# A gated cross-attention block with experts: units in three runs, four score tiles each with one maximum, then the full-precision products together; output weights in one load

## The chip, the cores and the metric

One core of a Trainium2 chip runs the whole kernel. The metric is the device time of one execution in microseconds (us); lower is better. Before the change three executions took 336.08, 337.61 and 337.05 us, median 337.05 us.

## The reference

The block has two halves. The first is cross-attention from 8 x 56 query tokens (width 128) to 8 x 1500 context tokens, with 16 heads of width 8, behind a layer norm and a tanh gate:

```
q = norm(x) @ w_q.T ; k = ctx @ w_k.T ; v = ctx @ w_v.T      # 16 heads of 8
attn = softmax(q k^T * 8**-0.5) ; out = (attn v) @ w_o.T
x = x + tanh(g_xattn) * out
```

The second is a mixture of 8 experts (inner width 512), of which a router picks two for every token; all eight are computed for all 448 tokens and combined with weights that are zero for the others:

```
probs = softmax(h @ gate_w.T) ; top 2, renormalised -> combine
gu = h @ gate_up_w ; out = sum_e combine_e * (up_e * gelu(gate_e)) @ down_e
x = x + tanh(g_ffn) * out
```

Everything is float32. The softmax of the first half needs the maximum of each (query, head) row, which the kernel computes by products of its own.

## The kernel before, in words

The kernel is written by hand for the five engines, each with its own program, tied by semaphores. There is no scheduler: the order on an engine is the order of the code.

**Units.** Attention works in 16 units, u = 0 to 15: a batch b (8 of them) times a half h of the heads (8 heads each). A unit has 12 score tiles of 128 keys; a tile is 128 x 448 (8 heads x 56 queries), made by two matmuls of 224 columns each (L880, `score_ps`), from keys `kx` as weights and block-diagonal queries `qx`. Keys and queries are split in a high and a low part in a rounded format (fp32r), stacked over the rows, so that one fast matmul does what three would. Rows 96 to 103 of `qx` carry the negated maxima against rows of ones in `kx`, so the score matmul subtracts the maximum.

**What an instruction is.** `scores` makes score tiles; in this version two tiles (a pair) per step. `max_scores` (L905) makes one of the 12 products of a unit, 112 query rows x 512 keys, from which `take_max` on VectorE (L664) takes the row maximum. After 12 of them `negate_max` (L670, L672, L674) makes `neg_max_parts`, `transpose_max` (L928) on TensorE transposes them, and `max_rows` (L683) on VectorE writes them to `qx`. `exp_pair` (L480) on ScalarE does the exponential of a pair (896 columns) to `probs`. `attend` (L919) multiplies four tiles of `probs` with the values: 16 matmuls, each in two passes of the trace (x32), in full precision (fp32), four heads side by side in 32-column groups of the array. `o_copy` (L488) takes the sum of a unit out of PSUM to `o_sb`, `denominators` (L936) spreads the sums of the exponentials, `invert` (L691) inverts them, and `normalise` (L377, GpSimd) multiplies. `project` (L862 for keys, L868 for values) does a third of the key or value projection of a batch that comes later, in full precision, through the one bank `misc_ps`; ScalarE evacuates it (L459 and L462 for keys, L474 for values) and GpSimd makes the low part of the keys (L351, `k_rest`).

**Work ahead.** While unit u is scored and attended, the maxima of unit u+1 are finished and those of unit u+2 begun. All products for maxima, the transpose and the denominators go through a ring of two PSUM banks, `max_ps`: a turn waits until VectorE has taken the turn two before it (`next_bank`). Four banks hold scores (two pairs), one `o_ps`, one `misc_ps`.

**Keys move.** The projected keys of a batch are moved by 12 DMAs from SP's queue (`move_keys`, L230) to two slots of `kx`, six per unit, when all three parts of `k_low` are done (L273) and the unit that used the slot has been scored. ScalarE waits in `keys_moved` for these copies before it overwrites `k_high` and `k_full` with the next batch's keys. In the prologue ScalarE's queue issues six of them. The output weights `wo_sb` are zeroed on VectorE (L700) and filled by 16 DMAs from GpSimd's queue (L370).

**The end.** Units 12 to 15 are unrolled; 13 to 15 have no projections, 14 no later maxima, 15 none. Between units 13 and 14 stands `project_out` of three quarters of the tokens (L1060). After unit 15 come the output projection of the rest, the router and the experts.

Of the kernel before, what the change touches and what calls it, by code (L numbers as in the profile page):

```python
# [33 lines left out]
PAIRS = KT // 2  # L34
TRIOS = KT // 4
UM = NCH * HP
RING = UM + 2
RING0 = UM + 6
# [19 lines left out]
def flamingo_block(nc, x, ctxT, g_attn, g_ffn, wqT, wkT, wvT, woT, gwT, guT, dnT, out):  # L58
# [3 lines left out]
    with ExitStack() as stack:  # L62
# [20 lines left out]
        probs = sb("probs", [128, 4, 2, SC // 2])  # L83
# [56 lines left out]
        hact = probs[:, 0:2, :, :].rearrange("p a b t -> p (a b) t")  # L140
# [9 lines left out]
        q_banks = [max_ps[:, 0, :], max_ps[:, 1, :], score_ps[:, 3, :], o_ps[:, :]]  # L150
        token_banks = [misc_ps[:, D * r:D * r + D] for r in range(NR)]
        xT_ps = max_ps[:, 0, :]
        gate_banks = [score_ps[:, 0, :], score_ps[:, 1, :]]
        up_banks = [score_ps[:, 2, :], misc_ps[:, :], score_ps[:, 3, :]]
# [9 lines left out]
        consts, mask_ready, select_all, cleared, wo_cleared, pool_step = map(sem, ("consts", "mask_ready", "select_all", "cleared", "wo_cleared", "pool_step"))  # L164
# [70 lines left out]
        def _(sp):  # L235
# [21 lines left out]
            sp.dma_start(kx[MR:KR, 0, 1, :].bitcast(f32), kx[MR:KR, 0, 0, :].bitcast(f32)).then_inc(ones_moved, 16)  # L257
            ones_rows(1)
# [6 lines left out]
            move_unit(1, 1)  # L265

            def body(i, par, ctx_next=True):
# [5 lines left out]
                sp.wait_ge(scores_done, PAIRS * (2 * b + 1))  # L273
                move_unit(par, 0)
                sp.wait_ge(scores_done, PAIRS * (2 * b + 2))
# [21 lines left out]
        def _(pool):  # L297
# [66 lines left out]
            pool.wait_ge(wo_cleared, 1)  # L364
            for s in range(2):
                for i in range(2):
                    for j in range(4):
                        h = 2 * (4 * s + j) + i
                        r = 32 * j + HD * i
                        pool.dma_start(wo_sb[r:r + HD, 2 * s + i, :], woT[HD * h:HD * h + HD, :]).then_inc(wo_loaded, 16)  # L370

            def normalise(i, par, h, turn=RING - 1):

# [8 lines left out]
            def body(i, par):  # L382
                b = batch(i, par)
                pool.wait_ge(scores_done, PAIRS * 2 * b + 1)
                stage(b + 1, 1 - par, 1)
                k_rest(b + 2, 0)
                normalise(i, par, 0)
                k_rest(b + 2, 1)
                k_rest(b + 2, 2)
                pool.wait_ge(scores_done, PAIRS * (2 * b + 1))  # L390
                stage(b + 2, par, 0)
                normalise(i, par, 1)
# [4 lines left out]
            pool.wait_ge(scores_done, PAIRS * (NU - 4) + 1)  # L397
# [18 lines left out]
            normalise(3, 1, 0, 8)  # L416
            for made, (kind, e) in enumerate(FIRST_WEIGHTS[:-1]):
                if made == 2:
                    normalise(3, 1, 1, 9 - RING)
                weights_rest(kind, e, e % 2, made + 1)  # L420
# [26 lines left out]
        def _(act):  # L447
# [6 lines left out]
            nc.scalar.activation(scratch[:, :], scratch[:, :], ACT.Exp).then_inc(exp_done, 1)  # L454
# [21 lines left out]
            def exp_pair(i, par, h, k):  # L476

                act.wait_ge(scores_done, PAIRS * unit(i, par, h) + k + 1)
                slot, bank = (PAIRS * h + k) % 4, 2 * (k % 2)
                nc.scalar.activation(probs[:, slot, :, :], score_ps[:, bank:bank + 2, 0:SC // 2],  # L480
                                     ACT.Exp, scale=SCALE).then_inc(exp_done, 1)

            def o_copy(i, par, h):

                u = unit(i, par, h)
                act.wait_ge(o_norm_ready, u + 1)
                act.wait_ge(pv_done, TRIOS * (u + 1))
# [20 lines left out]
            act.wait_ge(g_loaded, 32)  # L508
# [712 lines left out]
```

## Time and profile before

| | us |
|---|---|
| median of three executions | 337.05 |
| the profiled execution | 337.0 |
| its span | 335.3 |
| TensorE busy with matmuls | 294.7 (88%) |
| TensorE busy with weight loads | 223.0 (67%) |
| VectorE busy | 236.3 (70%) |
| ScalarE busy | 183.0 (55%) |
| GpSimd busy | 101.3 (30%) |

The span runs from the first to the last recorded instruction; the profiled execution's time is 1.7 us longer. TensorE's busy time counts a matmul from its start to its modelled end, so that one matmul's time overlaps the next; the step from start to start, or the chain of waits, says what a group of matmuls really takes. In the chain, every piece is the work or the wait that the next piece stood behind, so its pieces add up to the time that passed.

### The profile page before, as it was taken

To read this page: it belongs to the slowest core of one execution; us is meant where nothing else is said; L and a number is where in the kernel's file an instruction comes from. 1 tells how busy PE (TensorE), PEld (TensorE's weight loads), DVE (VectorE), ACT (ScalarE), POOL (GpSimd) and SP (SyncE) were. 2 spreads that over 40 slices of the span, in tenths; PEclk is the share of its full clock that TensorE was granted. 3 is DMA by queue.
4 is the path that set the end of the run, shared out by engine and by line. 5 is a ranking of instruction groups with operands and counts; after the bars stand their busy time and mean duration, and the time that the engine had idled before them with its cause. 6 is when DMAs were issued, how large, how long until landed. Compare 5 with 4: busy or idle time off the path is not lost.

```text
span 335.3 us, 7712 instructions
## 1 busy us (share of the span) xinstructions
PE 294.7 (88%) x2793; PEld 223.0 (67%) x2793; DVE 236.3 (70%) x429; ACT 183.0 (55%) x284; POOL 101.3 (30%) x124
## 2 busy tenths in 40 slices
PE   0949799999999999999999999898668899999875
PEld 0535586686686686687687686676556688887653
DVE  3534778778777778777777778866233788888874
ACT  1512367566566566566665664445616577775422
POOL 6021952311411411321320330000441066664330
PEclk9985899999999999999999999999956999999979
DMA  5498572197098098099087079300000000000000
GB/s 161 137 225 100 142 179 96 24 212 230 6 214 243 0 206 254 0 196 254 13 182 187 0 170 262 129 0 2 2 0 1 2 1 0 0 0 0 0 0 29
DMA packets 10379, 32.33 MB, mean 96 GB/s; under 512 B 2976, under 2 KB 3616, under 8 KB 10360
## 3 DMA queue, kind: packets, MB, share of 16 engines
q1 hardware_dynamic: 8840, 30.59, 36.8%
q10 hardware_dynamic: 1008, 1.42, 1.8%
q8 instruction: 12, 0.20, 0.2%
q0 software_dynamic: 512, 0.07, 0.1%
q14 instruction: 7, 0.06, 0.1%
HBM read 13.06 MB, written 0.23 MB: 40 GB/s over the span
## 4 chain that ended last, share of the span: by engine, by line
PE 67%; DVE 20%; issue 4%; POOL 2%; ACT 2%; DMA 2%; ACTq 1%; DVEq 0%; SPq 0%
PE max_ps L905 17%; PE o_ps L919 13%; DVE part_max L664 10%; PE score_ps L880 9%; PE misc_ps L868 5%; PE score_ps L1105 4%; PE misc_ps L862 3%; PE score_ps L1106 3%; PE score_ps L1107 3%; PE score_ps L862 2%; DVE kx L829 2%; DVE k_low L810 2%; DMA ctx_sb<-in_ctxT 2%; DVE probs L824 2%; POOL kx L404 1%
## 5 line engine op out<-in xcount | busy, mean ns | idle before, releaser
L664 DVE TENSOR_REDUCE part_max<-max_ps 112x1 f32<-112x512 f32 (+1 forms) x192 | 127.9, 674 | 53.9 <-PE max_ps L905 50.4
L480 ACT ACTIVATE probs<-score_ps 128x896 f32<-128x896 f32 x96 | 87.5, 918 | 52.2 <-PE score_ps L880 50.9
L905 PE MATMUL max_ps<-kx,qx 96*112 96x512 f32 (+1 forms) x192 | 92.7, 487 | 8.8 <-DVE part_max L664 7.2
L880 PEld LDWEIGHTS score_ps<-qx,kx 104*128 104x128 f32 (+1 forms) x384 | 56.4, 191 | 6.0 <-ACT probs L480 2.3
L880 PE MATMUL score_ps<-qx,kx 104*128 104x224 f32 (+1 forms) x384 | 59.8, 279 | 0.6 <-ACT probs L480 0.3
L351 POOL TENSOR_TENSOR k_low<-k_full,k_high 128x512 fp32r<-128x512 f32 (+1 forms) x21 | 26.2, 1251 | 110.2 <-ACT k_full L462 110.2
L905 PEld LDWEIGHTS max_ps<-kx,qx 96*112 96x112 f32 x192 | 34.5, 181 | 30.4 <-DVE part_max L664 25.4
L919 PE MATMUL o_ps<-probs,v_sb 128*32 128x112 f32 (+1 forms) x1536 | 46.6, 262 | 0.0
L919 PEld LDWEIGHTS o_ps<-probs,v_sb 128*32 128x32 f32 (+1 forms) x1536 | 35.3, 110 | 11.0 <-issue 9.1
L404 POOL TENSOR_TENSOR kx<-gu_sb,kx 128x512 fp32r<-128x512 f32 x16 | 23.1, 1446 | 38.4 <-ACT kx L562 38.4
L596 ACT ACTIVATE kx<-probs 128x448 fp32r<-128x448 f32 x32 | 18.5, 577 | 23.4 <-DVE probs L824 22.7
L868 PE MATMUL misc_ps<-wv_sb,ctx_sb 128*128 128x128 f32 x192 | 28.0, 293 | 3.2 <-ACT v_sb L474 3.2
L868 PEld LDWEIGHTS misc_ps<-wv_sb,ctx_sb 128*128 128x128 f32 x192 | 27.2, 207 | 5.3 <-ACT v_sb L474 4.1
L829 DVE TENSOR_TENSOR kx<-probs,kx 128x448 fp32r<-128x448 f32 x32 | 23.1, 721 | 0.3
L566 ACT ACTIVATE v_sb<-score_ps 128x448 f32<-128x448 f32 x32 | 17.2, 540 | 7.5 <-PE score_ps L1107 7.1
L824 DVE TENSOR_TENSOR probs<-score_ps,v_sb 128x448 f32<-128x448 f32 x24 | 14.9, 620 | 8.9 <-PE score_ps L1107 8.9
L474 ACT ACTIVATE v_sb<-misc_ps 128x512 f32<-128x512 f32 x24 | 14.4, 599 | 10.0 <-PE misc_ps L868 10.0
L862 PE MATMUL misc_ps<-ctx_sb,wk_sb 128*128 128x512 f32 (+1 forms) x38 | 19.0, 580 | 0.0
L377 POOL TENSOR_TENSOR o_norm<-o_sb,inv_den 128x112 f32 (+1 forms) x16 | 6.7, 421 | 39.2 <-DVE inv_den L691 39.2
L223 POOL TENSOR_TENSOR qx<-q_parts,head_mask 96x448 fp32r<-96x448 f32 x15 | 13.9, 931 | 10.5 <-DVE q_parts L710 10.2
L691 DVE RECIPROCAL inv_den<-max_ps 128x112 f32<-128x112 f32 x16 | 13.6, 849 | 4.6 <-PE max_ps L936 4.4
L488 ACT ACTIVATE o_sb<-o_ps 128x112 f32<-128x112 f32 x16 | 4.2, 263 | 21.3 <-PE o_ps L919 21.3
(148 smaller groups left out, 388.6 us busy)
## 6 DMA issues: line engine op xcount, KB each, us to landing
kx<-k_high SPq DMA_DIRECT2D x56, 187.5 KB, 3.9
ctx_sb<-in_ctxT SPq DMA_DIRECT2D x7, 750.0 KB, 6.3
kx<-k_low SPq DMA_DIRECT2D x28, 187.5 KB, 4.0
gu_sb<-in_guT SPq DMA_DIRECT2D x8, 512.0 KB, 4.7
dn_sb<-in_dnT SPq DMA_DIRECT2D x8, 256.0 KB, 5.3
kx<-k_high ACTq DMA_DIRECT2D x4, 187.5 KB, 5.5
ctx_sb<-in_ctxT SPq DMA_DIRECT2D x2, 256.0 KB, 6.7
kx<-k_high SPq DMA_DIRECT2D x4, 123.5 KB, 4.6
```

The costliest lines, as they stand in the source:

```text
L351: nc.gpsimd.tensor_tensor(k_low[:, start:start + size], k_full[:, start:start + size], k_high[:, start:start + size].bitcast(f32), ALU.sub ...
L404: nc.gpsimd.tensor_tensor(weight_parts[:, kind, par, 1, :], weights_of(kind, e), weight_parts[:, kind, par, 0, :].bitcast(f32), ALU.subtra ...
L480: nc.scalar.activation(probs[:, slot, :, :], score_ps[:, bank:bank + 2, 0:SC // 2], ACT.Exp, scale=SCALE).then_inc(exp_done, 1)
L596: nc.scalar.activation(hact_parts[:, j, 0, :], hact[:, j, :], ACT.Copy).then_inc(hact_high, 1)
L664: nc.vector.reduce_max(part_max[:, p, c:c + 1], max_ps[0:PC, bank, 0:size], AX.X).then_inc(max_taken, 1)
L824: nc.vector.tensor_tensor(hact[:, j, :], up_banks[j % NB][:, 0:TOK], gelu_sb[:, par, j, :], ALU.mult).then_inc(hact_full, 1)
L829: nc.vector.tensor_tensor(hact_parts[:, j, 1, :], hact[:, j, :], hact_parts[:, j, 0, :].bitcast(f32), ALU.subtract).then_inc(hact_ready, 1)
L862: nc.tensor.matmul(bank[:, 0:size], wk_sb[:, :], ctx_sb[:, par, start:start + size], start=True, stop=True).then_inc(k_done, 1)
L868: last = nc.tensor.matmul(misc_ps[:, 128 * k:128 * k + 128], ctx_sb[:, par, 128 * t:128 * t + 128], wv_sb[:, :], start=True, stop=True)
L880: last = nc.tensor.matmul(score_ps[0:m, t % 4, GC * g:GC * g + GC], kx[0:KR, 2 * par + h, g, 128 * t:128 * t + m], qx[0:KR, par, 2 * h + g ...
L905: nc.tensor.matmul(max_ps[0:PC, bank, 0:size], qx[0:MR, par, 2 * h + p // 2, PC * (p % 2):PC * (p % 2) + PC], kx[0:MR, slot, p // 2, start ...
L919: last = nc.tensor.matmul(o_ps[32 * j:32 * j + 32, PC * h:PC * h + PC], v_sb[0:m, par, t, VP * p:VP * p + 32], probs[0:m, (PAIRS * h + t / ...
```

## The change

In the loop of attention, each unit is now three runs. A run is four times (one score tile, one maximum product), then the full-precision products: a third of a projection, and the attend of the four tiles. The denominators of the unit before stand behind the first run, the transpose of the maxima of unit u+1 in the second, between projection and attend. The maxima of unit u+2 that are made ahead are six instead of five. Score tiles are counted one by one (`exp_tile` on ScalarE, 448 columns), with three score banks instead of two pairs; the maximum ring has three banks instead of two, so a turn waits for the turn three before it. `probs` keeps eight tiles, as before. The transpose counts for two turns, so the ring stays a multiple of three (15 turns per unit instead of 14).

Projections stand elsewhere: the last two value parts of batch b+1 in runs 1 and 2 of the even unit, key parts 0, 1, 2 of batch b+2 in run 3 of the even unit and runs 1 and 2 of the odd one, and the first value part of b+2 in its run 3. On GpSimd `stage` and one `k_rest` come ahead of `normalise`. In the prologue the keys of the second unit are moved from SP's queue, not ScalarE's, value projections stand later, and the first key projections of batch 1 use the three score banks. The output weights arrive already laid out (the zeros included, made on the host from the same matrix) and are one DMA of SP's queue.

```
-PAIRS = KT // 2
+RUN = 4
+RUNS = KT // RUN
-RING = UM + 2
+AHEAD = UM // 2
+RING = UM + 3
...
-        score_ps = pb("score_ps", [128, 4, 512])
-        max_ps = pb("max_ps", [128, 2, 512])
+        score_ps = pb("score_ps", [128, 3, 512])
+        max_ps = pb("max_ps", [128, 3, 512])
...
-            def exp_pair(i, par, h, k):
+            def exp_tile(i, par, h, t):
+                act.wait_ge(scores_done, KT * unit(i, par, h) + t + 1)
+                nc.scalar.activation(probs[:, (KT * h + t) % 8, :], score_ps[:, t % 3, 0:SC // 2],
                                      ACT.Exp, scale=SCALE).then_inc(exp_done, 1)
...
             def attention(i, par, h, after=True):                       # VectorE
-                for n in range(5, UM):
-                    take_max(ring(u, n - 5), (n - 5) % 2, n)
-                negate_max(u + 1, ring(u, UM - 5))
+                for n in range(RUN):
+                    take_max(ring(u, n), n % 3, AHEAD + n)
+                invert(u - 1, 1 - h, ring(u, RUN), RUN % 3)
+                for n in (5, 6):
+                    take_max(ring(u, n), n % 3, AHEAD + n - 1)
+                negate_max(u + 1, ring(u, 7))
...
-            def scores(i, par, h, k, rows=0):
+            def scores(i, par, h, t, rows=0):                            # TensorE
+                pe.wait_ge(exp_done, KT * unit(i, par, h) + t + FIRST_EXP - 2)
...
             def next_bank(turn):
-                pe.wait_ge(max_taken, turn - 1)
+                pe.wait_ge(max_taken, turn - 2)
...
+                scores(i, par, h, 0, rows)
+                next_max(6, 0)
+                scores(i, par, h, 1)
+                next_max(7, 1)
+                scores(i, par, h, 2)
+                next_max(8, 2)
+                scores(i, par, h, 3)
+                next_max(9, 3)
+                denominators(u - 1, 1 - h, ring(u, RUN), RUN % 3)
+                job(0)
+                attend(i, par, h, 0)
+                scores(i, par, h, 4)
+                next_max(10, 5)
+                scores(i, par, h, 5)
+                next_max(11, 6)
+                scores(i, par, h, 6)
+                later_max(0, 7)
+                scores(i, par, h, 7)
+                later_max(1, 8)
+                job(1)
...
+                    transpose_max(u + 1, ring(u, 9), 0, turns=2)
                 attend(i, par, h, 1)
+                for t in range(2 * RUN, KT):
+                    scores(i, par, h, t)
+                    later_max(t - 6, t + 3)
+                job(2)
                 attend(i, par, h, 2)
...
-                act.wait_ge(k_low_saved, NCH)
-            for g in range(2):
-                move_keys(act, 1, 1, g, (0, TK), kx_loaded[1][g])
...
+            sp.dma_start(wo_sb[:, :, :], wo).then_inc(wo_loaded, 16)
```

TensorE's order in the loop before the change, second half of an even unit. `REGISTER_ALU` computes the value of a wait; one row of x4 score matmuls is a pair of tiles, `max_ps<-kx,qx` is a maximum, `o_ps<-probs,v_sb` an attend, `misc_ps` a projection:

```order
L919 MATMUL o_ps<-probs,v_sb 32x112 x16
L892 REGISTER_ALU
L905 MATMUL max_ps<-kx,qx 112x476
L880 MATMUL score_ps<-qx,kx 128x224 x2
L880 MATMUL score_ps<-qx,kx 92x224 x2
...
L905 MATMUL max_ps<-kx,qx 112x512
L946 REGISTER_ALU
L868 MATMUL misc_ps<-wv_sb,ctx_sb 128x128 x4
L926 ISA
L892 REGISTER_ALU
L928 MATMUL max_ps<-ident,neg_max_parts 8x112
```

One or two maxima stand between any two full-precision products here. After the change, a whole run (the second of the first odd unit in the loop), with L871 a score tile, L891 a maximum, L854 a key projection, L914 the transpose and L905 the attend:

```order
L871 MATMUL score_ps<-qx,kx 128x224 x2
L878 REGISTER_ALU
L891 MATMUL max_ps<-kx,qx 112x512
L868 REGISTER_ALU
L871 MATMUL score_ps<-qx,kx 128x224 x2
...
L938 ISA
L854 MATMUL misc_ps<-ctx_sb,wk_sb 128x476
L912 REGISTER_ALU
L878 REGISTER_ALU
L914 MATMUL max_ps<-ident,neg_max_parts 8x112
L900 REGISTER_ALU
L905 MATMUL o_ps<-probs,v_sb 32x112 x16
```

The rounded products stand four and four together, and projection, transpose and attend follow each other.

VectorE's order in the loop before, from the last maximum of unit u+1 on:

```order
L664 TENSOR_REDUCE part_max<-max_ps 112x1 [waits max_done]
L670 TENSOR_REDUCE neg_max<-part_max 112x4 [waits max_taken]
...
L674 TENSOR_TENSOR neg_max_parts<-neg_max,neg_max_parts 112x4 [waits nm_step]
L676 REGISTER_ALU
L663 REGISTER_ALU [waits nm_step]
L664 TENSOR_REDUCE part_max<-max_ps 112x1 [waits max_done]
L680 REGISTER_ALU
L683 TENSOR_TENSOR qx<-max_ps,pair_mask 8x448 [waits max_done]
```

and after, in the same place (L653 is the maximum, L672 writes the transposed maxima to `qx`):

```order
L663 TENSOR_TENSOR neg_max_parts<-neg_max,neg_max_parts 112x4
L665 REGISTER_ALU
L652 REGISTER_ALU [waits nm_step]
L653 TENSOR_REDUCE part_max<-max_ps 112x1 [waits max_done]
L652 REGISTER_ALU
L653 TENSOR_REDUCE part_max<-max_ps 112x1 [waits max_done]
L669 REGISTER_ALU
L672 TENSOR_TENSOR qx<-max_ps,pair_mask 8x448 [waits max_done]
```

Two maxima instead of one now stand between the negation and the write to `qx`, and the denominators' inverse has moved from the unit's end to the place behind the first four maxima of the next unit.

## Rows read from the trace of the kernel before

**Rows 1.** The page: TensorE's granted clock in 40 slices, tenths of full speed

```profile
PEclk9985899999999999999999999999956999999979
```

**Rows 2.** Timeline of ScalarE, ends of units: start us, us, what [idle before]

```profile
52.11 0.26 ACT L488 ACTIVATE o_sb<-o_ps 128x112 f32<-128x112 f32 x1 [1.44 <-PE o_ps L919]
...
193.36 0.26 ACT L488 ACTIVATE o_sb<-o_ps 128x112 f32<-128x112 f32 x1 [1.09 <-PE o_ps L919]
...
218.27 0.26 ACT L488 ACTIVATE o_sb<-o_ps 128x112 f32<-128x112 f32 x1 [2.21 <-PE o_ps L919]
...
231.67 0.26 ACT L488 ACTIVATE o_sb<-o_ps 128x112 f32<-128x112 f32 x1 [1.24 <-PE o_ps L919]
...
239.73 0.26 ACT L488 ACTIVATE o_sb<-o_ps 128x112 f32<-128x112 f32 x1 [1.26 <-PE o_ps L919]
```

**Rows 3.** Chain of waits within one unit: start us, us, what

```profile
142.99 0.89 PE misc_ps L868 x8
...
147.29 0.44 PE score_ps L880 x4
147.73 0.22 PE max_ps L905
147.95 0.90 PE o_ps L919 x32
148.85 0.42 PE max_ps L905
...
153.42 0.49 PE max_ps L905
```

**Rows 4.** The page, section 5: weight loads of the maximum products, idle time before them

```profile
L905 PEld LDWEIGHTS max_ps<-kx,qx 96*112 96x112 f32 x192 | 34.5, 181 | 30.4 <-DVE part_max L664 25.4
```

**Rows 5.** Busy us in 129.18:141.99 and 141.99:154.88, two units; sum and mean

```profile
sum 25.70, PE 24.88 PEld 18.76 DVE 19.67 ACT 16.31 POOL 6.37; mean PE 12.44 PEld 9.38 DVE 9.83 ACT 8.15 POOL 3.19
```

**Rows 6.** Timeline of TensorE in unit 14

```profile
223.45 0.38 PE L905 MATMUL max_ps<-kx,qx 96*112 96x476 f32 x1
223.66 0.60 PE L880 MATMUL score_ps<-qx,kx 104*128 104x224 f32 x4
...
226.58 0.49 PE L905 MATMUL max_ps<-kx,qx 96*112 96x512 f32 x1
226.91 0.60 PE L880 MATMUL score_ps<-qx,kx 104*128 104x224 f32 x4
```

**Rows 7.** Timeline of VectorE in one unit

```profile
157.63 0.85 DVE L691 RECIPROCAL inv_den<-max_ps 128x112 f32<-128x112 f32 x1
...
164.80 0.17 DVE L670 TENSOR_REDUCE neg_max<-part_max 112x4 f32<-112x12 f32 x1
...
165.49 0.69 DVE L664 TENSOR_REDUCE part_max<-max_ps 112x1 f32<-112x512 f32 x1
166.21 0.62 DVE L683 TENSOR_TENSOR qx<-max_ps,pair_mask 8x448 fp32r<-8x448 f32 x1
```

**Rows 8.** Timeline of ScalarE: activations of 448 columns, two in a row and one alone

```profile
252.66 0.98 ACT L566 ACTIVATE v_sb<-score_ps 128x448 f32<-128x448 f32 x2
254.78 0.54 ACT L566 ACTIVATE v_sb<-score_ps 128x448 f32<-128x448 f32 x1 [1.14 <-PE score_ps L1107]
```

**Rows 9.** SP's DMA issues of one batch's keys, first and last; page, median landing

```profile
142.29 0.52 SPq L230 DMA_DIRECT2D kx<-k_high  x1
...
151.18 0.94 SPq L230 DMA_DIRECT2D kx<-k_high  x1
...
kx<-k_high SPq DMA_DIRECT2D x56, 187.5 KB, 3.9
```

**Rows 10.** Timelines of ScalarE and GpSimd: a key copy, the low part of keys

```profile
156.78 0.60 ACT L459 ACTIVATE k_high<-misc_ps 128x512 fp32r<-128x512 f32 x1 [0.18 <-PE misc_ps L862]
...
166.67 1.20 POOL L351 TENSOR_TENSOR k_low<-k_full,k_high 128x476 fp32r<-128x476 f32 x1 [4.32 <-ACT k_full L462]
```

**Rows 11.** Timeline of the prologue: weight loads of a value projection

```profile
22.48 1.78 PEld L868 LDWEIGHTS misc_ps<-wv_sb,ctx_sb 128*128 128x128 f32 x8 [3.47 <-ACT v_sb L474]
```

More of the change, by code:

```diff
@@ L362, in _, with normalise @@
                 k_rest(1, n)
[L364 to L372, printed above, removed]
+            def normalise(i, par, h, turn=RING + RUN):
                 u = unit(i, par, h)
@@ L543, in attention @@
                 o_copy(i, par, h)
-                if not last:
-                    exp_pair(*ahead(i, par, h, 1), 0)
-                if job_next:
-                    evacuate(*ahead(i, par, h, 1), 0)
             with act.Fori(0, B // 2 - 1) as i:
@@ L657, in k_rest, with take_max @@
                                         ).then_inc(k_low_saved, 1)
-            def take_max(turn, bank, n, first=False):
+            def take_max(turn, bank, n, first=False, turns=1):
                 p, c = max_product(n, first)
@@ L676, in negate_max, with max_rows @@
                 dve.wait_ge(nm_step, 3 * v + 3)
-            def max_rows(turn, bank, par, h):
+            def max_rows(turn, bank, par, h, turns=1):
                 dve.wait_ge(max_done, turn + 1)
@@ L723, in _ @@
             for n in range(UM):
-                take_max(n, n % 2, n, first=True)
+                take_max(n, n % 3, n, first=True)
             negate_max(0, UM)
             take_max(UM, 0, 0)
-            max_rows(UM + 1, 1, 0, 0)
-            for n in range(1, 5):
-                take_max(UM + 1 + n, (n + 1) % 2, n)
+            take_max(UM + 1, 1, 1)
+            max_rows(UM + 2, 2, 0, 0)
+            for n in range(2, AHEAD):
+                take_max(UM + 1 + n, (1 + n) % 3, n, turns=3 if n == AHEAD - 1 else 1)
             nc.vector.tensor_copy(expert_sel[:, :, :], bc(row_mask[:, :].unsqueeze(2), [16, E, 128])).then_inc(select_all, 1)
@@ L902, in max_scores @@
                     pe.wait_ge(kx_loaded[slot][n // 6], MOVES * (i + 1))
-                if not first or n >= 2:
+                if not first or n >= 3:
                     next_bank(turn)
@@ L1012, in attention @@
+            transpose_max(0, UM + 2, 2)
+            for n in range(2, AHEAD):
+                max_scores(0, 0, 1, n, UM + 1 + n, (1 + n) % 3, turns=3 if n == AHEAD - 1 else 1)
+            pe.wait_ge(k_saved, 4 * NCH)
+            pe.wait_ge(ones_moved, 64)
+            def attention(i, par, h, rows, jobs=(0, 1, 2), after=True):
                 u = unit(i, par, h)
                 u1, u2 = ahead(i, par, h, 1), ahead(i, par, h, 2)
-                def next_max(n):
-                    max_scores(*u1, n, ring(u, n - 5), (n - 5) % 2)
@@ L1044, in attention @@
[L1044 to L1054 removed]
+                        max_scores(*u2, n, ring(u, turn), turn % 3)
@@ L1199, with heads_apart @@
     layout = np.ascontiguousarray
+    def heads_apart(rows):
+        blocks = np.zeros((4, 32, 4, D), np.float32)
+        for s in range(2):
+            for i in range(2):
+                for j in range(4):
+                    h = 2 * (4 * s + j) + i
+                    blocks[j, HD * i:HD * i + HD, 2 * s + i] = rows[HD * h:HD * h + HD]
+        return blocks.reshape(128, 4, D)
     arrays = {
```

317 lines of the change are left out of this document (141 added, 176 removed).

## The prediction, made before the change was run

> **What bounds the kernel now.** I read the page's busy shares and clock first, then the timeline of ScalarE for the unit boundaries, then the chain of waits through one unit, then the timelines of TensorE, VectorE and ScalarE around it, and last the DMA queue. TensorE is busy for 88% of the span, VectorE 70%, ScalarE 55%, as the table above has it; the clock row stands at 9 from the sixth slice up to the end of attention, the full 2.4 GHz level but for a few us [rows 1]. The copy of a unit's output (o_sb) marks its end: 16 units, of which five are shown: 0, 11, 13, 14 and 15, at 52.11, 193.36, 218.27, 231.67 and 239.73 us [rows 2]. From unit 0 to unit 11 lie 11 periods in 141.25 us: **12.84 us per unit**. What follows the last copy (335.3 - 239.7 = 95.6 us: router, experts, store) is hardly touched. The profiled execution took 337.0 us, 1.7 us more than its span, and stands at the median of 337.05.
>
> Where do 12.84 us go? I add TensorE's own work in a unit from the chain of waits [rows 3], where a step is the time until the next can follow:
> - six score pairs at 0.44: 2.64
> - twelve maxima at 0.23: 2.76
> - three attends (o_ps x32) at 0.90: 2.70
> - three projections at 0.89 (the key ones 0.86): 2.61
> - behind each attend the next product takes 0.42 and not 0.23, since its weight load is not hidden: 3 x 0.19 = 0.57
> - transpose and denominators, about 0.2 each: 0.4
>
> Sum 11.7 us. The other **1.15 us are TensorE waiting for VectorE**: a maximum that comes back from such a wait stands in the chain with 0.49 instead of 0.23, as in its last row [rows 3], and page section 5 names the waiter: weight loads of L905 idled 30.4 us in all, 25.4 of it for part_max L664, that is 25.4 / 16 = 1.6 us per unit with the ends [rows 4]. VectorE is not full: 9.83 us busy in a unit [rows 5]. It waits for TensorE and TensorE for it in turns, because two maximum banks hold only one product ahead, and because the negation (three small steps) is followed by one more maximum and the transpose in the same narrow place.
>
> **The change, run by run.** A unit becomes three runs of four (score tile, maximum), each followed by the full-precision products, as the two excerpts of TensorE's order show. TensorE's columns stay what they were: the same 24 score matmuls, 12 maxima, 3 projections, 3 attends. Price of one (tile, maximum): 0.22 + 0.23 = 0.45; the one place where a maximum stands between scores on both sides shows it (223.45 to 223.66 for a 476-column maximum, then 0.44 for four score matmuls) [rows 6]. So a run is 4 x 0.45 = 1.8, plus 0.19 behind the attend ahead of it, plus 0.88 projection, plus 0.90 attend, plus 0.2 in two of three runs: again 11.7 us.
>
> The waits, walked. A maximum takes VectorE 0.69 [rows 7], a little less for 476 columns, 0.67 on average; I estimate that it starts about 0.2 after its product's last column.
> - Run 1: products end at 0.6, 1.1, 1.5, 2.0; VectorE is free of them at 1.5, 2.1, 2.8, 3.5. The denominators need the second bank: wait 0.1 to 0.2. invert 0.85 [rows 7] ends at 4.3, beside projection and attend (until 4.2).
> - Run 2: two maxima until 6.2, then the negation: 0.17 three times with gaps, 0.7 from 164.80 to 165.49 [rows 7], until 6.9. TensorE reaches the transpose at 6.9: wait 0 to 0.1. Then two maxima until 8.2 and max_rows 0.62 [rows 7] until 8.9, beside the attend.
> - Run 3: begins at about 8.1; its second maximum needs the bank of the transpose, free at 8.9, and comes at 9.0. The last maxima are taken by 11.5, before run 1 fills again.
>
> Waits 0.3 us instead of 1.15: **12.0 us per unit**, a gain of 0.84. VectorE's 9.83 us of work would fill 82% of that, so it doesn't bound.
>
> ScalarE: twelve exps of 448 columns instead of six of 896. Alone, 448 columns take 0.54 and two in a row 0.98, so the second adds 0.44 [rows 8]. Per unit that is 5.3 to 6.5, with the copies some 3 more, in 12: ScalarE is busy 8.15 now [rows 5] and becomes no bound. The attend waits for the fourth exp of its run, at 0.4 + 4 x 0.54 = 2.6 in the worst case; TensorE gets there at 2.0 + 0.88 = 2.9. The projection hides it. Where there is no projection, it doesn't (below).
>
> Key copies: L230 moves begin when k_low is done, 12 DMAs, first 142.29, last 151.18, and 3.9 us to land: 12.8 us [rows 9]. In the new order the last key chunk is projected at 6.9 of the odd unit, copied (0.6 + 0.5) and rounded on GpSimd (1.2 [rows 10]) by about 9.2; the copies land at 22.0. ScalarE needs them ahead of the next key copy at about 10.3 + 12 = 22.3. That is 0.3 us of slack plus roughly 0.8 that ScalarE can be late before TensorE feels it. I cost it at nothing and keep its price as a rival.
>
> Units without projections (13, 14, 15): TensorE stalls at each attend for exps, but has 2.6 less work. Unit 13: run = 0.4 + 4 x 0.45 (exp) + 0.1 + 0.90 + 0.2 = 3.4, and VectorE 9.8 over all; about 11.0. Unit 12 still has two projections: 11.8. The two took 24.9 (193.36 to 218.27): -2.1. Unit 14 has only six maxima, and the output projection: about 12.6 against 13.4: -0.8. Unit 15 had score pairs running ahead of the attends and took 8.06 [rows 2]; now scores 4 to 7 stand behind attend 0, so each run is 3.2 to 3.3: 9.6, **+1.5**.
>
> Prologue: ScalarE issued six key DMAs ahead of the first value copy, and TensorE idled 3.47 for that copy until 22.48 [rows 11]. That goes, but the keys of the first unit still have to land, and the clock's half level (1.2 GHz, the 8, 5 and 8 in the third to fifth slice [rows 1]) covers the same work. I take -1.0, bounds -3 and +1.5 (the second unit's keys now queue on SP behind the first's, six issues of 0.5 to 0.9 as in [rows 9]). The 16 wo_sb DMAs leave GpSimd's queue; what stood behind them, a qx that is read two units later, has time: nothing, at most -0.5. The one DMA in their place stands on SP behind 12 key moves, ahead of the first ctx load in the loop: one issue, nothing.
>
> **Sum**: -1.0 (prologue), 11 x -0.84 = -9.2, -2.1, -0.8, +1.5: together -11.6. 337.0 - 11.6 = 325.4 profiled, and as median **325.4 us**. Its own bounds: the waits 0 to 0.6 per unit (13 units: -4 to +4), the prologue: 321 to 329.5.
>
> **A rule against the row.** The chain shows 0.42 behind an attend against 0.23 behind scores [rows 3], an exposed weight load. The Trainium skill, "TensorE: Matmul & The Clock Gate", section "Step-by-step: what each phase is for", says that TensorE pulls the next weight load ahead of matmuls still in flight. Here the trace disagrees at the seam behind an attend and agrees within a run of scores and maxima (0.21 to 0.23). By the rule alone a border would cost nothing.
>
> **Rivals.**
> - *Loads hide at the new borders.* Behind an attend now come scores, not a maximum, and nothing in the trace shows that pair. If the 0.19 goes: 13 x 0.57 = 7.4 less, 318 us. Against: the seam shows after every attend and the load's form is alike. 7%. (The skill's rule above would give this.)
> - *Keys arrive late.* The copies land over 1 us later than I think, ScalarE stops in front of the key copy, and exps of the next unit come late. For: slack of about 0.3 against 1.7 now (landed 155.1, key copy at 156.78 [rows 9, 10]). Up to 0.4 us per unit: 330 us. 16%.
> - *The gain does not come.* The third bank only moves the waiting (VectorE's chain negation, transpose, max_rows stands in each unit as before), unit 12.7 to 12.85, with +1.5 at the end: 336 to 338. Against: VectorE idles 3 us per unit now. 7%.
> - *Slower.* Every score tile behind a maximum pays the exposed load. In the timeline most such steps are 0.33 (226.58 to 226.91) and only 223.45 to 223.66 is 0.21 [rows 6]. If 0.33 is the rule, 12 x 0.10 = 1.2 per unit, 13.2 against 12.84: 13 x 0.36 = +4.7, +1.5 in the last unit, -3 elsewhere: 340 us. It decides if the step is over 0.29. Against: the 0.33 ones follow a full-precision product, whose price I have counted. 8%.
>
> **How the numbers follow.** Forecast 62% (325.4, own range 321 to 329.5), keys late 16% (330), hidden loads 7% (318), no gain 7% (337), slower 8% (340). A measurement tells about 0.5% (1.7 us) from no change. Faster: 62 + 16 + 7, and 2 of the 7 without gain: 0.87. Same 0.05. Slower 0.08. The range 319.5 to 331.5 leaves out the last two cases and half of the hidden loads.
>
> **What would show it.** Copies of o_sb 11.7 to 12.3 us apart; weight loads of the maxima idle under 8 us for part_max in all; a tile and its maximum 0.45 apart; exps of 0.44 to 0.54; the last unit at 9 to 10 us; key copy on ScalarE not released by a DMA. The forecast is wrong if periods are over 12.5, if scores behind a maximum inside a run come 0.3 later, or if ScalarE waits for kx.

## The result, and the profile after

The changed kernel took **330.72 us** (median of four, 330.35 to 331.68), the kernel before beside it 336.66 (four, 336.08 to 337.61): ratio **0.985 (0.981 to 0.988)**. Forecast were 325.4 us, so about half of the forecast gain came. The ratios below leave out executions that took over 1.5% longer than the fastest of the same kernel.

The profiled execution took 331.7 us, the longest of the four; its span is 329.9. First the copies that end units 0, 11, 12, 13, 14 and 15, from ScalarE's timeline (start us, us, what); they answer to [rows 2].

```profile
52.48 0.27 ACT L486 ACTIVATE o_sb<-o_ps 128x112 f32<-128x112 f32 x1
...
184.82 0.26 ACT L486 ACTIVATE o_sb<-o_ps 128x112 f32<-128x112 f32 x1 [0.28 <-PE o_ps L905]
...
196.58 0.26 ACT L486 ACTIVATE o_sb<-o_ps 128x112 f32<-128x112 f32 x1 [1.16 <-PE o_ps L905]
...
207.37 0.26 ACT L486 ACTIVATE o_sb<-o_ps 128x112 f32<-128x112 f32 x1 [1.16 <-PE o_ps L905]
...
220.50 0.26 ACT L486 ACTIVATE o_sb<-o_ps 128x112 f32<-128x112 f32 x1 [1.16 <-PE o_ps L905]
...
231.89 0.26 ACT L486 ACTIVATE o_sb<-o_ps 128x112 f32<-128x112 f32 x1 [0.81 <-PE o_ps L905]
```

By stages, from these and [rows 2] (profiled executions, us):

| stage | before | after | difference | forecast |
|---|---|---|---|---|
| up to the copy of unit 0 | 52.11 | 52.48 | +0.4 | -1.0 |
| units 1 to 11 | 141.25 | 132.34 | -8.9 | -9.2 |
| units 12 and 13 | 24.91 | 22.55 | -2.4 | -2.1 |
| unit 14 | 13.40 | 13.13 | -0.3 | -0.8 |
| unit 15 | 8.06 | 11.39 | +3.3 | +1.5 |
| last copy to the span's end | 95.6 | 98.0 | +2.4 | 0 |
| sum | 335.3 | 329.9 | -5.4 | -11.6 |

The loop did what was forecast; both ends of the program took back 6 us (+0.4, +3.3 and +2.4 in the table). The loop first: the chain of waits within one unit (start us, us, what), answering to [rows 3].

```profile
166.87 0.89 PE misc_ps L860 x8
167.76 0.19 PE max_ps L914
167.96 0.86 PE o_ps L905 x27
168.82 0.41 PE score_ps L871 x2
169.24 0.22 PE max_ps L891
169.46 0.22 PE score_ps L871 x2
```

The chain is all TensorE now. Two score matmuls behind an attend take 0.41, behind a maximum 0.22, and a maximum takes 0.23. The page's section 5 (busy, mean ns, then the idle time before, with its releasers) answers to [rows 4]:

```profile
L891 PEld LDWEIGHTS max_ps<-kx,qx 96*112 96x112 f32 x192 | 34.3, 180 | 5.3 <-issue 2.2 <-DMA kx<-k_high 0.9 <-DVE part_max L653 0.7
...
L921 PEld LDWEIGHTS max_ps<-o_sb,den_sel 128*128 128x128 f32 x34 | 5.7, 204 | 5.7 <-DVE part_max L653 3.6 <-issue 1.3 <-ACT o_sb L486 0.7
```

Where the maxima waited 25.4 us for part_max, they wait 0.7. What is left stands in front of the denominators, 3.6 us over 16 units, 0.2 in each. The busy times of the two units 148.5 to 160.6 and 160.6 to 172.7, as in [rows 5]:

```profile
sum 24.20, PE 24.12 PEld 18.80 DVE 18.56 ACT 16.91 POOL 6.37; mean PE 12.06 PEld 9.40 DVE 9.28 ACT 8.45 POOL 3.19
```

TensorE is busy for 12.06 of 12.10 us. Its busy time counts modelled ends (it was 12.44 of 12.85 before, with 1.15 of waits), so the stronger sign is the chain: from 160.56 to 173.97 it holds TensorE's pieces and 0.04 us beside them. TensorE is the bound of the loop.

### The profile page after: what moved, and what is told of

The parts are those of the page before. It is cut to its first block, busy times and chain, and to the rows that moved or that the text cites. A ratio compares the mean times of both kernels' runs of the same rounds, so it can differ in the third digit from the quotient of the medians.

```text
span 329.9 us, 7978 instructions
## 1 busy us (share of the span) xinstructions
PE 288.1 (87%) x2795; PEld 222.9 (68%) x2795; DVE 229.3 (69%) x430; ACT 187.5 (57%) x380; POOL 92.6 (28%) x108
## 4 chain that ended last, share of the span: by engine, by line
PE 67%; DVE 10%; DMA 5%; SPq 5%; ACT 4%; issue 4%; POOL 2%; DVEq 0%; ACTq 0%; POOLq 0%
PE score_ps L871 13%; PE o_ps L905 12%; PE max_ps L891 11%; PE misc_ps L860 5%; SPq L234 5%; PE misc_ps L854 4%; PE score_ps L1097 3%; DMA kx<-k_high 3%; PE score_ps L1098 2%; PE score_ps L1099 2%; ACT probs L478 2%; DVE kx L821 2%; DVE k_low L802 2%; DMA ctx_sb<-in_ctxT 2%; PE max_ps L921 2%
## 5 line engine op out<-in xcount | busy, mean ns | idle before, releaser
L653 DVE TENSOR_REDUCE part_max<-max_ps 112x1 f32<-112x512 f32 (+1 forms) x192 | 118.8, 672 | 46.1 <-PE max_ps L891 43.6
L478 ACT ACTIVATE probs<-score_ps 128x448 f32<-128x448 f32 x192 | 91.7, 544 | 35.8 <-PE score_ps L871 34.2
L871 PE MATMUL score_ps<-qx,kx 104*128 104x224 f32 (+1 forms) x384 | 77.7, 288 | 7.1 <-DMA kx<-kx 5.3
L871 PEld LDWEIGHTS score_ps<-qx,kx 104*128 104x128 f32 (+1 forms) x384 | 67.4, 190 | 21.9 <-issue 13.5
L891 PE MATMUL max_ps<-kx,qx 96*112 96x512 f32 (+1 forms) x192 | 78.3, 413 | 1.6 <-DMA kx<-k_high 0.6
L905 PE MATMUL o_ps<-probs,v_sb 128*32 128x112 f32 (+1 forms) x1536 | 47.8, 262 | 3.2 <-ACT probs L478 3.2
L905 PEld LDWEIGHTS o_ps<-probs,v_sb 128*32 128x32 f32 (+1 forms) x1536 | 36.3, 109 | 15.4 <-ACT probs L478 9.7
L891 PEld LDWEIGHTS max_ps<-kx,qx 96*112 96x112 f32 x192 | 34.3, 180 | 5.3 <-issue 2.2
L860 PEld LDWEIGHTS misc_ps<-wv_sb,ctx_sb 128*128 128x128 f32 x192 | 24.6, 192 | 1.7 <-ACT v_sb L473 0.7
L860 PE MATMUL misc_ps<-wv_sb,ctx_sb 128*128 128x128 f32 x192 | 25.5, 276 | 0.2 <-ACT v_sb L473 0.2
L458 ACT ACTIVATE k_high<-misc_ps 128x512 fp32r<-128x512 f32 (+1 forms) x18 | 10.6, 587 | 13.8 <-PE misc_ps L854 11.6
L854 PE MATMUL misc_ps<-ctx_sb,wk_sb 128*128 128x512 f32 (+1 forms) x36 | 18.1, 584 | 0.0
L227 POOL TENSOR_TENSOR qx<-q_parts,head_mask 96x448 fp32r<-96x448 f32 x15 | 13.9, 930 | 14.0 <-DVE q_parts L698 11.6
L816 DVE TENSOR_TENSOR probs<-score_ps,v_sb 128x448 f32<-128x448 f32 x16 | 10.0, 622 | 8.9 <-PE score_ps L1099 8.9
```

The costliest lines, as they stand in the source:

```text
L478: nc.scalar.activation(probs[:, (KT * h + t) % 8, :], score_ps[:, t % 3, 0:SC // 2], ACT.Exp, scale=SCALE).then_inc(exp_done, 1)
L653: nc.vector.reduce_max(part_max[:, p, c:c + 1], max_ps[0:PC, bank, 0:size], AX.X).then_inc(max_taken, turns)
L854: nc.tensor.matmul(bank[:, 0:size], wk_sb[:, :], ctx_sb[:, par, start:start + size], start=True, stop=True).then_inc(k_done, 1)
L860: last = nc.tensor.matmul(misc_ps[:, 128 * k:128 * k + 128], ctx_sb[:, par, 128 * t:128 * t + 128], wv_sb[:, :], start=True, stop=True)
L871: last = nc.tensor.matmul(score_ps[0:m, t % 3, GC * g:GC * g + GC], kx[0:KR, 2 * par + h, g, 128 * t:128 * t + m], qx[0:KR, par, 2 * h + g ...
L891: nc.tensor.matmul(max_ps[0:PC, bank, 0:size], qx[0:MR, par, 2 * h + p // 2, PC * (p % 2):PC * (p % 2) + PC], kx[0:MR, slot, p // 2, start ...
```

## The experiments

Each ran beside the kernel before on the same chip. Ratios are to that kernel, with their 95% interval.

**The changed kernel again.**

> The changed kernel again, beside the others on the same chip. Both theories: 329 to 332 us, periods of 12.1 us between output copies, last unit 11.4, 98 us behind the last output copy. What it tells: whether the half-speed stretches of TensorE's clock behind attention (232 to 249 and 256 to 259 us in the first trace) come back in the same places. If the second one is a matter of chance, it is missing or elsewhere here and the time behind the last copy is about 95.5 us.

330.89 us, ratio 0.986 (0.980 to 0.991). Period 12.10 and last unit 11.38 repeat to a few hundredths, the first copy (52.14) to 0.3. The part behind the last copy is 96.8 and not 98.0, so it varies between executions: the stretch at 1.2 GHz at 256 us is missing, and another stands at 313.7 to 320.6.

**Two maximum banks.** The new order, ring of two instead of three (RING, the turns and the waits all follow):

```
-                pe.wait_ge(max_taken, turn - 2)
+                pe.wait_ge(max_taken, turn - 1)
```

> Against the changed kernel: the ring for maxima, transpose and denominators has two PSUM banks instead of three (a turn waits for the turn two before it), 14 turns per unit; the order of the runs stays. Theory A (the third bank is what took TensorE's waits for VectorE away): within a run the third and fourth maximum wait for VectorE's 0.67 us each, about 2 x 0.2 per run and more at the start of runs, period 12.9 to 13.6 us instead of 12.1, total 340 to 350. Rival (the order does it, the bank adds little): period under 12.4, total under 336.

350.93 us, ratio **1.046 (1.038 to 1.054)**; period 13.67, both a little above the upper ends that theory A gave. Its row answers to that of L891 above:

```profile
L891 PEld LDWEIGHTS max_ps<-kx,qx 96*112 96x112 f32 x192 | 34.3, 180 | 21.8 <-DVE part_max L653 14.4 <-issue 3.0 <-DMA kx<-k_high 0.6
```

So the third bank carries the gain, 1.57 us per unit in this order; grouping with two banks loses 0.83 against the order before (12.84). No run has three banks in the order before, so what the grouping itself adds to the third bank is not shown.

**Projections inside the runs.** Behind the second maximum of each run rather than between the run's last maximum and the attend:

```
                 scores(i, par, h, 1)
                 next_max(7, 1)
+                job(0)
                 scores(i, par, h, 2)
...
                 denominators(u - 1, 1 - h, ring(u, RUN), RUN % 3)
-                job(0)
                 attend(i, par, h, 0)
```

(the other two likewise)

> Against the changed kernel: each run's projection stands in its middle, behind two (tile, maximum) pairs, so it is apart from the attend; all else stays. If every border from full precision to rounded products costs an exposed weight load, three more borders at 0.19 make the period 12.4 to 12.7 us and the total 335 to 340. If only the border behind an attend costs it, the projection in the middle costs nothing and lets VectorE catch up: period 11.9 to 12.1, total 328 to 331.

336.36 us, ratio 1.002 (0.999 to 1.005), period 12.67. The size is in the range that the text gives for dearer borders, but the chain gives another cause:

```profile
132.74 0.80 PE misc_ps L854 x2
133.54 0.22 PE score_ps L871 x2
...
134.24 0.55 ACT probs L478
...
134.84 0.97 PE o_ps L905 x32
135.81 0.41 PE score_ps L871 x2
```

Scores behind a projection take 0.22: that border is free. What costs is the attend, which now stands behind the fourth exponential of its run (0.55 of ScalarE in the chain, 10.7 us of attend idle for ScalarE in all where there were 3.2; the difference over the 13 units with projections is 0.58 in each, the rise of the period). The projection ahead of the attend is the cover of that exponential. Of my two stated outcomes the first had the number with the wrong cause, the second the right premise (only the border behind an attend costs) with the wrong number, because it left this wait out.

**Output weights by 16 DMAs of GpSimd again,** and VectorE's zeroing of them:

```
-            sp.dma_start(wo_sb[:, :, :], wo).then_inc(wo_loaded, 16)
...
+                        pool.dma_start(wo_sb[r:r + HD, 2 * s + i, :], wo[r:r + HD, 2 * s + i, :]).then_inc(wo_loaded, 16)
```

> Against the changed kernel, one part undone: the output weights are zeroed on VectorE and filled by 16 DMAs from GpSimd's queue (8.9 us of it), not by one load from SP's. Forecast's theory: nothing to see, within 0.5 us of 331, since nothing waits for GpSimd there. Rival: the queries of unit 3 and the low keys of batch 2 behind the 16 DMAs come late, first output copies 1 to 3 us later.

329.73 us, ratio 0.982 (0.976 to 0.988), first copy 51.67 against 52.1 to 52.5. The time is 1.2 below the changed kernel's beside the first runs, more than the 0.5 expected, but the intervals of the ratios overlap: no gain of the one load is seen, as forecast.

**Ones rows first.** The four DMAs of ones rows ahead of all key moves on SP's queue:

```
             sp.dma_start(ctx_sb[:, 1, 0:TK], ctxT[1]).then_inc(ctx_loaded[1], 16)
+            sp.wait_ge(kx_ones, 1)
+            sp.dma_start(kx[MR:KR, 0, 1, :].bitcast(f32), kx[MR:KR, 0, 0, :].bitcast(f32)).then_inc(ones_moved, 16)
+            ones_rows(1)
+            ones_rows(2)
+            ones_rows(3)
...
             move_unit(0, 1)
-            ones_rows(1)
-            ones_rows(2)
-            ones_rows(3)
```

> Against the changed kernel: the four DMAs that copy the rows of ones are issued right behind the context loads, ahead of every key move. Theory A (keys bind the start): the 5.3 us in which TensorE waits for the ones go, scores begin near 34 us instead of 37.1, but ScalarE still stands in front of the third batch's key copy until the second batch's key moves have landed (51.3 us), so the first output copy comes at 51.5 to 52.3 and the time falls by 0 to 1 us. Theory B (the ones rows are what the start lost): the first output copy comes at about 49 and the time falls by 3 us or more.

The reason for it, in the changed kernel: SP's issues (first), and TensorE's first scores.

```profile
25.97 0.94 SPq L234 DMA_DIRECT2D kx<-k_high  x1
26.95 3.88 SPq L246 DMA_DIRECT2D kx<-kx  x3
```

```profile
31.39 0.44 PE L891 MATMUL max_ps<-kx,qx 96*112 96x476 f32 x1 [0.29 <-DVE part_max L653]
37.14 0.76 PE L871 MATMUL score_ps<-qx,kx 104*128 104x224 f32 x2 [5.31 <-DMA kx<-kx]
```

The second unit's keys were put on SP (22.19 to 26.9) in front of the ones rows, and the score matmuls need those: 5.3 us of TensorE. With the ones rows first, the same row becomes

```profile
32.88 0.48 PE L871 MATMUL score_ps<-qx,kx 104*128 104x224 f32 x2
```

and the first copy comes at 47.65 instead of 52.48. Theory B holds, theory A falls: ScalarE's copy of the third batch's keys was to stay until 51.3, but the moves that it waits for come earlier too (issued from 33.58 instead of 36.05), and it stands at 46.68 instead of 51.51. The time followed less: 328.17 us (325.13 to 332.67), and 327.42 without the longest of the four, ratio 0.973 (0.964 to 0.982): 3.5 us below the changed kernel beside it, for 4.8 in the first copy. Of the profile's 4.8, unit 1 takes 0.5 back (11.82 for 11.36) and unit 15 1.5 (12.88 for 11.39): in that unit TensorE works at 1.2 GHz from 222.4 to 225.8, where the changed kernel had the full level.

**The second unit's keys on ScalarE's queue,** as before:

```
-            move_unit(0, 1)
...
+            act.wait_ge(k_low_saved, NCH)
+            for g in range(2):
+                move_keys(act, 1, 1, g, (0, TK), kx_loaded[1][g])
```

> Against the changed kernel, one part undone: the key moves of the second unit are issued from ScalarE's queue, as before the change, and not from SP's ahead of the rows of ones. Theory A (the rows of ones were late only because they stood behind those six moves): scores begin at about 34 and not 37.1, but ScalarE's value copies come some 4 us later (as before the change) and TensorE idles for them near 20 us; first output copy at 49 to 51.5, total 1 to 3 us less than the changed kernel. Rival (the moves had to leave ScalarE's queue for the start to be any faster): first output copy at 52 or later, total the same or more.

First copy at 50.15 (-2.3), inside theory A's range, but 331.59 us, ratio 0.986 (0.980 to 0.993): no gain, where A had 1 to 3 us. Here too the clock row dips before the attention ends (the first of the two 7s ahead of the 5, 224.7 to 228.1 us, in unit 15), as it did not in the changed kernel:

```profile
PEclk9998799999999999999999999997759799999979
```

```profile
PEclk9999599999999999999999999999559799999979
```

(the variant first, the changed kernel second). Unit 15 takes 12.79 here and 12.88 with the ones rows first, for 11.39: time gained ahead of unit 1 was lost in the last unit in both. Why the level falls there in one execution and not in another stays open.

**Token transposes behind the third run's scores,** in unit 15:

```
-                    transpose_tokens(0, NR - 1, NR)
                     attend(3, 1, 1, 1)
+            transpose_tokens(0, NR - 1, NR)
             attend(3, 1, 1, 2)
```

> Against the changed kernel: only the six token transposes of the last unit move from before its second attend to before its third. If the transposes waiting for the layer norm (1.3 us idle in the trace) are what made the last unit 11.4 instead of my 9.6, it takes 9.9 to 10.2 us, and the total is 1.2 to 1.5 less. If the serial runs alone are the cause, it stays over 11.

326.69 us, ratio 0.973 (0.967 to 0.979); last unit 9.99, three equal runs of 3.33. The unit gave 1.4 as expected, the total 4. What the other 2.6 are isn't shown: the profile is that of the longest execution (329.8), where unit 1 takes 12.95 for 11.36, with a stretch at 1.2 GHz in it (53.7 to 57.1), and the part behind the last copy 96.1 for 98.0.

**Last unit's scores ahead of the attends** (the transposes late as well):

```
...
+            for t in range(KT):
+                scores(3, 1, 1, t, ring(NU - 2, TAIL) + 1)
+                if t == RUN - 1:
+                    denominators(NU - 2, 0, ring(NU - 2, TAIL + 1), (TAIL + 1) % 3)
+                if t == RUN + 2:
+                    attend(3, 1, 1, 0)
+                if t == 2 * RUN + 2:
+                    attend(3, 1, 1, 1)
+            transpose_tokens(0, NR - 1, NR)
...
```

> Against the changed kernel: in the last unit three score tiles run ahead of each attend (order: tiles 0 to 3, denominators, 4 to 6, attend, 7 to 10, attend, 11, token transposes, attend). Theory A (the exps and attends of the last unit stand in series, and the transposes in its middle wait for the layer norm): last unit 8.0 to 8.6 us instead of 11.4, total 2.8 to 3.5 us less. Rival: the end is set by the layer norm's chain or by ScalarE's exps alone (12 x 0.46 = 5.5 plus the ends), unit over 10 us, under 1 us gained.

326.4 us (325.75 to 326.73), ratio **0.970 (0.965 to 0.976)**; last unit 8.15, 3.2 less; the total is 4.5 below the changed kernel's beside it, and here too the rest lies behind the last copy (96.1 for 98.0 in the profiles), where executions differ. The changed kernel's chain in unit 15, from the second run on:

```profile
225.15 0.87 POOL rstd L412
...
226.04 0.45 DVE xn L628
...
226.54 0.99 PE max_ps L1055 x6
227.53 0.90 PE o_ps L905 x32
228.43 0.43 PE score_ps L871 x2
...
228.88 1.86 ACT probs L478 x4
...
230.78 1.02 PE o_ps L905 x32
```

and of the variant:

```profile
224.82 0.55 ACT probs L478
...
225.42 0.48 PE score_ps L871 x2
225.90 0.90 PE o_ps L905 x32
226.80 0.37 PE score_ps L871 x2
227.17 0.66 PE max_ps L1055 x6
227.84 0.99 PE o_ps L905 x32
```

Two things stood in the last unit: the run is serial, scores, four exponentials, attend (0.43 + 1.86 + 1.02 and gaps: 3.3 to 3.4 us), and the transposes waited in front of the second attend for a layer norm that passes through VectorE and GpSimd.

**Both repairs.** The two edits together.

> Both repairs in one kernel: the ones rows ahead of the second unit's keys on SyncE's queue (as in the run with the ones rows early), and unit 15's score tiles running ahead of the attends. If the two losses are separate: first o_sb copy at 47.7 us, period 12.10, last unit 8.2, sum against the changed kernel -4.6 - 3.2 = -7.8, so 322 to 323 us. Rival, the clock: the time saved in the prologue lets a stretch at 1.2 GHz fall elsewhere (as it fell in the sparse last units with the ones rows early alone, at 222.4 to 225.8, and gave only 2.7 us of the 4.6): then 324 to 326, with such a stretch between 190 and 235 us in the profile and a spread over 3 us among its runs. If denser last units keep the clock full until the last copy, no such stretch stands there and the first number holds.

First copy 48.34, period 12.10, last unit 8.15, span 322.9. The six executions spread from 320.83 to 329.89: three at a mean clock of 0.955 to 0.968 took 320.8 to 324.6 and give the ratio 0.954 (0.949 to 0.960); three at 0.945 to 0.950 took 328 to 330. The median of all six, 326.29, is no better than that of the last unit's repair alone. In the profiled execution, one of the quick three, the mechanism adds up: 7.0 us less span than the changed kernel, 7.8 expected. But the gain isn't reliable. The rival on the clock had the spread right. Its place isn't settled: this profile has no stretch at 1.2 GHz between 190 and 227, and none of the three long executions was profiled.

**Attends of units 13 and 14 two tiles later,** on top of both:

```
+                late = jobs == ()
+                if not late:
+                    attend(i, par, h, 0)
...
+                if late:
+                    attend(i, par, h, 0)
```

> As the run with both repairs, and in units 13 and 14, which have no projection to stand between a run's last score tile and its attend, the attend is moved two score tiles back, behind scores of the next run. Theory (the attend there waits 0.7 to 0.9 us for the fourth exp of its run): three such waits in unit 13, two or three in unit 14 go, as far as VectorE (9.8 us of work in unit 13) lets them: units 12 and 13 together 22.55 -> 22.0, unit 14 13.13 -> 12.2, total 1 to 1.5 us below the run with both repairs. Rival: VectorE's maxima and the negation bound these units, so that what goes from the attend comes back as waits for part_max: units 12 to 14 within 0.3 us of before, total within 0.5 us of the run with both repairs.

327.36 us median (322.50 to 331.14); its two quick executions, 322.50 and 322.51, are level with the quick three of both repairs (median 322.35). Unit 14 fell from 13.13 to 12.61, units 12 and 13 rose from 22.54 to 23.22, +0.2 together. The rival was right; the chain in unit 13:

```profile
195.26 0.84 DVE inv_den L679
196.10 1.11 DVE part_max L653 x2
197.23 0.18 DVE neg_max L659
```

Take the exponential away in front of the attend, and VectorE's inverse, maxima and negation bound a unit without projections.

**Behind the last copy.** Here the profiles count seven expert passes, from one `k_full` of VectorE to the next. In the changed kernel:

```profile
252.86 0.62 DVE L794 TENSOR_TENSOR k_full<-max_ps,xnT 128x448 f32<-128x448 f32 x1 [5.08 <-PE max_ps L1110]
260.53 0.62 DVE L794 TENSOR_TENSOR k_full<-max_ps,xnT 128x448 f32<-128x448 f32 x1 [1.39 <-PE max_ps L1110]
269.73 0.61 DVE L794 TENSOR_TENSOR k_full<-max_ps,xnT 128x448 f32<-128x448 f32 x1
277.86 0.62 DVE L794 TENSOR_TENSOR k_full<-max_ps,xnT 128x448 f32<-128x448 f32 x1
```

7.67, 9.20 and 8.13 us; before, the same three took 6.19, 8.14 and 8.11. The first holds a stretch at 1.2 GHz (255.9 to 259.3): +1.5. The run with the keys on ScalarE's queue has such a stretch there too and takes 7.68; in the twelve other traces the pass takes 6.15 to 6.19. The second holds one long instruction more than a pass of 8.13: +1.1. VectorE, and GpSimd beside it:

```profile
261.90 1.73 DVE L821 TENSOR_TENSOR kx<-probs,kx 128x448 fp32r<-128x448 f32 x1
...
271.10 0.61 DVE L821 TENSOR_TENSOR kx<-probs,kx 128x448 fp32r<-128x448 f32 x1
271.63 1.73 DVE L802 TENSOR_TENSOR k_low<-k_full,k_high 128x448 fp32r<-128x448 f32 x1
```

```profile
261.72 1.43 POOL L402 TENSOR_TENSOR kx<-gu_sb,kx 128x512 fp32r<-128x512 f32 x1 [5.75 <-ACT kx L551]
...
271.13 1.74 POOL L402 TENSOR_TENSOR kx<-gu_sb,kx 128x512 fp32r<-128x512 f32 x1 [4.46 <-ACT kx L551]
```

Where GpSimd's product began 0.18 ahead of VectorE's it took VectorE 1.73 instead of 0.61; where it began just behind, VectorE kept its time, and only the next one (`k_low`) was long, as it is in every pass but the first, before the change too. Before, two of seven passes took 9.2, now three; the two together, +2.5, are all of the tail's loss. To test it, GpSimd waits until VectorE is done with these products; the rest is the variant with the last unit's scores ahead:

```
                 made = 3 * e + 5 if split_gate else 2 * e + 10
+                pool.wait_ge(hact_ready, FT * e + FT)
                 weights_rest(UP, e + 1, 1 - par, made + 1)
```

> The tail. With the last unit's scores ahead, two of the seven expert passes shown by VectorE's x products (from one k_full to the next) take 9.20 us and the others 8.13; in the changed kernel three do. Theory: the 1.07 is one product of VectorE with two operands in SBUF (kx<-probs,kx), 1.73 us instead of 0.62, where GpSimd's product for the next expert's weights (L402) has begun just ahead of it. Here GpSimd waits in each pass until VectorE has finished these products of the expert. If that is so: no kx<-probs,kx over 0.7 us but those of the last expert, all passes 8.1 to 8.3, and the total 2 to 3 us below the kernel with the last unit's scores ahead (326.4), so about 324. Rival: GpSimd is then the late one (two or three weights of 1.3 to 1.7 us each behind the wait, 5 us of a pass of 8.1), its low parts come late for TensorE, and passes grow to 9 or more: total 326 or above.

> The kernel with the last unit's scores ahead, once more, as the yardstick for the run beside it: 326.4 us within 0.5, period 12.10, last unit 8.15. How many expert passes take 9.20 should depend on where GpSimd's product falls against VectorE's: two or three of seven.

**321.77 us** (321.27 to 323.26), ratio **0.958 (0.954 to 0.962)**; the yardstick beside it 326.04 (323.95 to 327.19), 0.970 (0.965 to 0.974). The same rows:

```profile
264.71 0.39 DVE L799 CAST k_high<-k_full 128x448 fp32r<-128x448 f32 x1
265.01 0.62 DVE L822 TENSOR_TENSOR kx<-probs,kx 128x448 fp32r<-128x448 f32 x1
265.55 0.62 DVE L803 TENSOR_TENSOR k_low<-k_full,k_high 128x448 fp32r<-128x448 f32 x1
```

```profile
265.91 1.42 POOL L402 TENSOR_TENSOR kx<-gu_sb,kx 128x512 fp32r<-128x512 f32 x1 [3.72 <-ACT kx L552]
```

No product of VectorE in the passes is long, k_low neither, and all passes behind the first take 8.2 to 8.3: a pass of 9.2 has gone for each long `kx` product, while passes in which only `k_low` was long took no more (8.13). From the first k_full to the last it gains 1.25 us (55.76 against 57.01). Another 1.05 lies between the last copy and the first k_full, ahead of every product that the new wait holds back, and 1.5 behind the last k_full. There the clock differs: one stretch at 1.2 GHz behind the attention (232.7 to 246.3) where the yardstick has three (230.7 to 247.8, 312.7 to 316.1, 322.9 to the end at 324.1). That the wait brought this about isn't shown, and no run has the wait in the changed kernel alone. That the total gained 4.3 us in six executions is shown, and more than the 2 to 3 expected. This is the best of the kernels here, 9 us below the changed one.

## Why the prediction was right in direction and wrong in size

The mechanism of the loop was right. What failed are three terms at the ends: what follows the last copy, put at nothing (off by 2.4 us), the last unit (1.8) and the prologue (1.4); unit 14 adds 0.5. That 330.7 lies close to the 330 of the rival "keys arrive late", and inside the wider range, is chance: that rival's wait is not in the loop.

**The loop, right.** Step "Where do 12.84 us go?": third bank and grouping should leave 12.0 per unit; 132.34 / 11 = 12.03, with unit 1 at 11.36 and a period of 12.10 behind it. The waits left are 0.2 (0.3 forecast). The sum of TensorE's own work was 11.7 and should be 11.9, so two small errors partly cancel.

**Units 12 and 13, right** (22.55 for 22.8). **Unit 14, off by 0.5:** its attends stand behind the exponentials and VectorE's chain; moving the one exposes the other.

**Last unit, mis-sized.** The step "so each run is 3.2 to 3.3: 9.6" had the runs nearly right (3.33, three of them 9.99 and not 9.6) and left out the transposes between them: 11.39. Late transposes gave 9.99 (-1.4). The term is +3.3, not +1.5, and it was avoidable: 8.15.

**Prologue, a wait left out.** It came out at +0.4, inside its bounds and not at -1.0. I credited the 3.47 us of [rows 11] and bounded SP's queue at +1.5, "the second unit's keys now queue on SP behind the first's". I named the six issues, but only asked who waits for them, not who waits for what stands *behind* them, the ones rows: 5.3 us of TensorE. With these rows first the first copy comes 4.5 us earlier than before the change.

**Tail, costed at nothing.** "What follows the last copy is hardly touched" is true of its instructions, not of its time: +2.4, of it 1.5 a stretch at 1.2 GHz that the repeat's profile didn't have there (its tail is 96.8, +1.2) and 1.1 a meeting of VectorE and GpSimd. I had no bound on it.

**The rivals.** Hidden loads: false, 0.41 behind every attend of the loop. The Trainium skill, "TensorE: Matmul & The Clock Gate", section "Step-by-step: what each phase is for", has the next weight load pulled ahead of running matmuls if it goes to the background buffer or other rows; behind a projection the trace with projections inside the runs agrees (0.22), behind an attend of 32-column tiles the traces here do not (0.41). Keys late: false in the loop. ScalarE's key copies idled 7.6 us for a DMA in all, on two occasions ahead of the first output copy: 5.4 until 30.78 and 2.2 until 51.51. Behind the second the exponentials came late and TensorE idled 1.0 at 53.24; the sign "if ScalarE waits for kx" came there, and nowhere behind. No gain: false with three banks. Slower by the price of scores behind a maximum: false, 0.22.

## What to carry to other kernels

When a transfer is moved on a queue, list what stands behind it up to the end of the queue, and who waits for each. Price the first and last unit of an unrolled loop instruction by instruction, with everything that is woven into them: the loop was right to 0.3 us here and the ends cost 6. And where a filler is moved, ask which wait it covered.

## What the runs showed of the hardware

- A product on VectorE with both operands in SBUF took 1.73 us instead of 0.62 when GpSimd's product of 128x512 had begun 0.18 us ahead of it. The Trainium skill, "GPSIMD Engine Reference", section "1. Specifications", says that GpSimd's SBUF interfaces are shared with VectorE and that instructions with two SBUF inputs contend; the trace agrees. In the changed kernel's, the four `kx` products that VectorE began 0.07 to 0.18 us behind GpSimd's took 1.72 or 1.73; three begun within 0.03 us of it kept 0.61 or 0.62, and GpSimd's took 1.74 to 1.80. In the repeat one begun 0.02 behind took 1.76, so the border lies there. VectorE's products that read PSUM kept 0.62 or 0.63 beside it. One wait to keep them apart made the passes 1.25 us shorter.
- Two score matmuls took 0.41 behind an attend (32-column tiles) and 0.22 behind a projection (128 columns), both of these in full precision.
- Earlier work does not always end earlier: of 4.8 us gained in the prologue 1.9 were lost again by the end of unit 15, 1.5 of them in a unit with a stretch at 1.2 GHz, and the four executions lay between 325.1 and 332.7 us.
